# Three cross attentions: stacked rounded parts for the scores, and exponentials made with keys in rows

## The reference

```
q = (x @ Wq + bq) -> [B, H=16, 112, 16]      k, v = ctx_768 @ Wk + bk, @ Wv + bv -> [B, 16, 375, 16]
attn = einsum('bhqd,bhkd->bhqk', q, k) * 16**-0.5
L0_xattn: attn = clip(attn, -10000, 10000)
L1_xattn: attn = where(mask, attn, -finfo.max)
attn = softmax(attn);  x = einsum('bhqk,bhkd->bqhd', attn, v);  out = x @ Wo + bo
L3_xattn: out = relu(x @ W1 + b1) @ W2 + b2
```

## Time and profile before

| | us |
|---|---|
| median of three runs | 1796.17 |
| the profiled execution, span from first to last instruction | 1785.6 |
| what lies around that span, against the median | 10.6 |
| TensorE busy | 1579.5 (88%) |
| TensorE weight loads busy | 1305.9 (73%) |
| VectorE busy | 941.3 (53%) |
| ScalarE busy | 717.5 (40%) |
| GpSimd busy | 409.0 (23%) |
| mean granted TensorE clock | 0.957 of 2.4 GHz |

### The profile page before, as it was taken

The page is one execution under the profiler, slowest core; times in us unless marked ns, Lnnn a source line. Parts: engine busy times, 40 slices in busy tenths (PEclk is TensorE's granted clock), DMA queues, the critical chain, the costliest instruction groups (busy, mean ns, idle before and its releaser), DMA issues.

```text
span 1785.6 us, 40853 instructions
## 1 busy us (share of the span) xinstructions
PE 1579.5 (88%) x14786; PEld 1305.9 (73%) x14786; DVE 941.3 (53%) x2546; ACT 717.5 (40%) x1675; POOL 409.0 (23%) x627
## 2 busy tenths in 40 slices
PE   7998998799987879998797788997988999899998
PEld 6876776678975657776687566775876777689897
DVE  3665877511116657777110562556345667565864
ACT  3334876232323336652222314551755556211110
POOL 2224776500004421112000233432121111000101
PEclk9998999999998999998899798998998999999999
DMA  5343000278951011102686001001001000033232
GB/s 212 147 151 121 28 27 19 106 279 300 321 185 35 1 53 44 29 15 87 254 290 228 13 1 58 28 27 48 1 1 66 23 26 15 24 96 117 81 108 68
DMA packets 41852, 166.72 MB, mean 93 GB/s; under 512 B 5985, under 2 KB 16865, under 8 KB 30177
## 3 DMA queue, kind: packets, MB, share of 16 engines
q1 hardware_dynamic: 39392, 159.14, 25.7%
q0 software_dynamic: 2304, 5.51, 1.0%
HBM read 140.21 MB, written 24.41 MB: 92 GB/s over the span
## 4 chain that ended last, share of the span: by engine, by line
PE 70%; DVE 12%; issue 7%; DMA 3%; POOL 3%; ACT 3%; SPq 1%; DVEq 0%; POOLq 0%; ACTq 0%
PE bank L1688 7%; PE bank L1701 6%; PE bank L1268 6%; PE bank L1630 4%; PE bank L1255 4%; PE bank L1631 4%; PE bank L1632 4%; PE bank L1282 3%; PE bank L795 2%; PE bank L804 2%; PE bank L1238 2%; PE bank L1243 2%; PE bank L896 1%; PE bank L782 1%; DMA xrow<-slots 1%
## 5 line engine op out<-in xcount | busy, mean ns | idle before, releaser
L2053 ACT ACTIVATE arena<-big,nm 112x375 f32<-112x375 f32 x384 | 215.9, 605 | 29.5 <-DVE nm L2894 16.4
L1268 PEld LDWEIGHTS bank<-cst,arena 112*125 112x125 f32 x1152 | 146.6, 192 | 54.0 <-issue 29.0
L1268 PE MATMUL bank<-cst,arena 112*125 112x112 f32 x1152 | 168.0, 283 | 8.8 <-ACT big L2063 5.0
L3150 POOL TENSOR_TENSOR mv<-mv,cst 112x1 f32<-112x1 f32 x88 | 20.1, 228 | 607.3 <-DVE mv L2283 607.3
L2202 ACT ACTIVATE htile<-bank,wup 128x128 f32<-128x128 f32 x280 | 79.7, 368 | 189.7 <-PE bank L1688 189.6
L1688 PE MATMUL bank<-xtile,wup 128*128 128x128 f32 x1120 | 132.8, 278 | 0.3 <-DVE xtile L2997 0.2
L1688 PEld LDWEIGHTS bank<-xtile,wup 128*128 128x128 f32 x1120 | 129.8, 194 | 1.0 <-DVE xtile L2997 0.9
L3013 DVE COPY yrow<-bank 128x256 f32<-128x256 f32 x35 | 14.8, 424 | 217.5 <-PE bank L1701 217.5
L1701 PE MATMUL bank<-wdn,htile 128*128 128x256 f32 x560 | 126.3, 379 | 0.0
L2897 DVE TENSOR_SCALAR_CACHE_REDUCE big<-bank 112x375 f32<-112x375 f32 x192 | 96.0, 543 | 35.3 <-PE bank L1255 33.6
L1701 PEld LDWEIGHTS bank<-wdn,htile 128*128 128x128 f32 x560 | 103.9, 190 | 12.8
(11 more groups left out here) (359 smaller groups left out, 3571.7 us busy)
## 6 DMA issues: line engine op xcount, KB each, us to landing
wup<-in_moe_up SPq DMA_DIRECT2D x35, 1028.0 KB, 7.3
wdn<-in_moe_dn SPq DMA_DIRECT2D x35, 1024.0 KB, 6.1
vspace<-in_ring SPq DMA_DIRECT2D x40, 512.0 KB, 4.2
ctxs<-parts SPq DMA_DIRECT2D x30, 564.0 KB, 3.9
slots<-mlpw SPq DMA_DIRECT2D x11, 1024.0 KB, 6.5
parts<-ctxs SPq DMA_DIRECT2D x8, 564.0 KB, 3.1
xrow<-slots SPq DMA_DIRECT2D x35, 128.0 KB, 5.0
slots<-yrow SPq DMA_DIRECT2D x35, 128.0 KB, 7.0
```

The costliest lines, as they stand in the source:

```text
L1268: mm = pe.transpose(bank[4 + (3 * g + t) % 2][0:KT, j * T:(j + 1) * T], c_pr[:, g, j, t * KT:(t + 1) * KT], ident[0:T, 0:T])
L2053: nc.scalar.activation(c_pr[:, g, j, :], c_sc[:, g % 2, j, :], ACT.Exp, bias=nm[:, p, h:h + 1], scale=-1.0).then_inc(cexp_done, 1)
```

## The change

For these three stages:

- Queries and keys are split into a rounded part (float32r) and the remainder. The rounded part is made by ScalarE (`q_high`, `k_high`), the remainder by GpSimd (`q_low`) and VectorE (`k_low`).
- SyncE copies the parts by DMA, on chip, into stacks with the four heads' 32 rows side by side in time and three blocks of rows: queries high, low, high against keys high, high, low. That is 12 transfers for the keys and 12 for the queries of each batch (13 for the keys with the mask, whose row is row 96).
- Scores are made twice. With queries in rows (L1338 in the new kernel): one float32r matmul of 96 or 97 rows for each head, two heads at a time into one pair of banks, only for the maxima (L2977, one reduce over 2 x 375). The maxima are split too, turned (L1347), and multiplied into rows 96 to 104 of the query stack (`joined`). With keys in rows (L1357): for each tile of 125 keys two float32r matmuls of 105 rows and 224 columns, which give scores minus maxima already turned.
- ScalarE takes the exponentials straight from PSUM (three of 125 x 448 for each group) to where the value products read them. The 12 transposes and the copies go.
- In the clip stage the exponentials are clipped to [exp(-60), 1], two tiles by GpSimd and one by VectorE.
- The keys and values of batch b + 1 and the queries of b + 2 are made in batch b; those of batch 0 all come before the first scores. The copy of the output out of PSUM goes from VectorE to ScalarE. A value product now belongs to `back[2]`, not `back[3]`.
- GpSimd fills constant rows of the stacks at the start of each stage (9 x 3008 twice, with the mask also 1 x 1792 twice).

Core of the diff (the moved order of the steps is shown by rows below it):

```diff
+            def stack_keys(sub, b, p):
+                sp.wait_ge(ckl_done, at(sub, "k2", b, 2))
+                sp.wait_ge(ct_ready, at(sub, "c12", b - 2, 12))
...
+                for i in range(4):
+                    for r, part in enumerate((0, 0, 1)):
+                        sp.dma_start(k_st[32 * r:32 * r + 32, p, :, :]....bitcast(F32),
+                                     k_hl[32 * i:32 * i + 32, part, :, :].bitcast(F32)).then_inc(kst_in, 16)
...
+                if not sub.qk_norm:
+                    stack_keys(sub, 0, 0)
+                    stack_queries(sub, 0, 0)
                 next_weights(SUBS[sub.index - 1])
...
+                    if not sub.qk_norm:
+                        stack_queries(sub, b0 - 1, 1)
                     load_context(sub, b0, 0, False)
+                    if not sub.qk_norm:
+                        stack_keys(sub, b0 - 1, 1)
+                        stack_queries(sub, b0, 0)
...
-                def scores(b, g, p):
...
-                        rows = slice(32 * j, 32 * j + 32)
-                        pe.matmul(bank[j][0:T, 0:S2], c_qm[rows, p, g // 2, g % 2, :], c_kT[rows, p, g // 2, :],
-                                  start=True, stop=True).then_inc(cs_ready, 1)
+                def scores(b, g, p, half):
+                    if g == 0 and half == 0:
+                        pe.wait_ge(qst_in, queries_stacked(sub, b))
+                        pe.wait_ge(kst_in, keys_stacked(sub, b))
+                    pe.wait_ge(cmax_ready, at(sub, "p8", b, 2 * g + half))
+                    for e in range(2):
+                        mm = pe.matmul(bank[e][0:T, 0:S2P], q_st[0:rows, p, 2 * g + half, e * T:(e + 1) * T],
+                                       k_st[0:rows, p, 2 * g + half, :], start=True, stop=True)
+                    mm.then_inc(cs_ready, 1)
+                def shifts_t(b, g, p):
...
+                    pe.transpose(bank[2][:, 0:T], x_nm[:, g % 2, :].bitcast(F32), ident[0:T, 0:T]).then_inc(cx_ready, 1)
+                def scores_t(b, g, p, t):
...
+                    pe.wait_ge(cexp_done, at(sub, "c12", b, n - 1))
+                    for k in range(2):
+                        mm = pe.matmul(bank[4 + n % 2][0:KT, 2 * T * k:2 * T * (k + 1)], k_st[0:SHIFTS, p, 2 * g + k, t * KT:(t + 1) * KT],
+                                       q_st[0:SHIFTS, p, 2 * g + k, :], start=True, stop=True)
...
+                def exps(b, g, p, t):
...
+                    nc.scalar.activation(x_pt[:, g % 2, t, :], bank[4 + n % 2][0:KT, 0:4 * T], ACT.Exp).then_inc(cexp_done, 1)
...
+                def maxima(b, g, half):
+                    dve.wait_ge(cs_ready, at(sub, "p8", b, 2 * g + half + 1))
+                    dve.tensor_reduce(nm[:, g % 2, 2 * half:2 * half + 2], pair[0:T, :, 0:S2], AX_X, ALU.max, negate=True)\
+                        .then_inc(cmax_ready, 1)
...
+                def joined(b, g, p):
+                    dve.wait_ge(cx_ready, at(sub, "g4", b, g + 1))
...
+                nc.gpsimd.memset(k_st[96:SHIFTS, 0, :, :].bitcast(F32), 1.0).then_inc(xset, 1)
```

More of the change, by code:

```diff
@@ L1359, in step @@
-                        if two and sub.mlp:
+                            if not one:
+                                pe.wait_ge(ckl_done, at(sub, "k2", b, 2))
+                            elif sub.mlp:
+                                pe.wait_ge(cq_done, at(sub, "c1", b + 1, 1))
+                            else:
+                                pe.wait_ge(cv_done, at(sub, "c3", b, 3))
+                            keys(b + 1, 1 - p, 0, bank[3])
+                    if g == 1 and more:
+                        pe.wait_ge(ckl_done, at(sub, "k2", b + 1, 1))
+                        keys(b + 1, 1 - p, 1, bank[3])
@@ new lines, in step @@
+                    if g == 2 and more:
+                        pe.wait_ge(ckl_done, at(sub, "k2", b + 1, 2))
+                        value_rows(b + 1, 1 - p, 0, bank[3])
+                    if g == 3:
+                        if more:
+                            pe.wait_ge(cv_done, at(sub, "c3", b + 1, 2 if sub.mlp else 1))
+                            value_rows(b + 1, 1 - p, 2 if sub.mlp else 1, bank[3])
+                        if two and one and not sub.mlp:
+                            idle(b, 2)
+                            pe.wait_ge(con_step, at(sub, "t2", b, 0))
+                            rows_t(sub, b - 2, p)
@@ L1360, in step @@
+                    if back[0]:
+                        scores(b, g, p, 1)
+                    if back[2] and not sub.clip:
+                        values(*back[2])
+                    if back[1]:
+                        scores_t(*back[1], 0)
+                        scores_t(*back[1], 1)
+                    if g == 0 and two:
+                        if not one:
+                            idle(b, 1)
+                        if sub.mlp:
                             hidden(b - 2)
-                        elif two:
-                            if not one:
-                                idle(b, 1)
+                        else:
@@ new lines, in step @@
+                        if after and not sub.mlp:
+                            if two:
+                                y_taken(b - 2)
+                            q_in(b + 2, TL)
+                    if g == 2:
+                        if one:
+                            idle(b, 2)
+                            if sub.mlp:
+                                if two:
+                                    y_taken(b - 2)
+                            elif after:
+                                pe.wait_ge(cq_done, at(sub, "c1", b + 2, 1))
@@ L1449, in step @@
-                        if back[3] and not sub.mlp:
-                            values(*back[3])
-                        if one and not sub.mlp:
-                            idle(b, 1)
-                            output_columns(sub, b - 1)
+                        if after and sub.mlp:
+                            pe.wait_ge(cv_done, at(sub, "c3", b + 1, 3))
+                            q_in(b + 2, bank[3])
+                    if back[2] and sub.clip:
+                        values(*back[2])
@@ L2923, in step @@
-                    if back[0]:
-                        scores_in(b, g, p, (0, 1))
+                    after = more and (not isinstance(b, int) or b + 2 < B)
+                    y_at = 2 if sub.mlp else 1
+                    if back[0]:
+                        maxima(b, g, 0)
+                    if back[1]:
+                        joined(*back[1])
+                    if back[2] and sub.clip:
+                        clipped(*back[2])
                     if two and g == 0 and sub.mlp:
                         output_columns(sub, b - 2)
-                    if two and g == y_at + 2:
+                    if two and g == y_at:
+                        residual(sub, b - 2, p)
@@ L2937, in step @@
[L2937 to L2944 removed]
+                        maxima(b, g, 1)
+                        shifts(b, g, p)
+                    if g < 2 and more:
+                        k_low(b + 1, 1 - p, g, bank[3])
```

699 lines of the change are left out of this document (359 added, 340 removed).

## The result

The changed kernel takes 1976.6 us (median of four runs) against 1795.9 for the kernel before: a ratio of 1.102, 95% interval 1.098 to 1.105. It is slower by 181 us where 14 less were forecast; the range ended at 1825. In the profiled executions the span went from 1785.6 to 1975.0.

A forecast was written before the change was run, and what follows sets the result against it. TensorE (88% busy) was taken to set the steady time, GpSimd the new clip stage; steady batches -45, starts +45 and ends -14 us gave -14 from 1796.2, so 1782 us, range 1750 to 1825.

The forecast's parts named there:

- TensorE's steady work: Steady batches: 2.4 us less where nothing else bounds, 1.4 from replaced matmuls and transposes, 1.0 from fewer waits.
- SyncE's queue: Steady part: 24 transfers a batch at 0.5 us an issue, between rows of 0.34 and 0.65, priced at nothing.
- the slack: Steady part: the next batch's keys need 8.5 us against two steps and a bit, 8.8.
- The starts: Starts of the three stages: first scores wait behind 24 issues, then batch 0 takes 15.4 us; +45 us in all.
- The ends: After each stage's last scores: a shorter chain, half the saving counted, 4.5 us each; -14, bounds -5 and -22.
- GpSimd's clip: Clip stage: 1.85 us for 448 columns, so GpSimd's 18.9 us a batch bounds it and the gain is 1.7.
- L3314's row: Old kernel's GpSimd profile row, 1545 ns for 375 elements with a pointer, used to price the new clip.
- Rival B: Next batch's scores wait for key stacks, transfers over 32 partitions getting half the rate; 1831 us, chance 0.19.
- its point of decision: Key transfers in the steady part: stacks come late from about 0.52 us for each transfer.
- Chances of 0.58 for faster: Whole kernel: faster 0.58, from the cheap-transfer case and most of the forecast; same 0.12, slower 0.30.

## Why the prediction was wrong, point by point

- **TensorE's steady work: the sum right, by luck.** Forecast 2.4 us less for a batch, 1.4 of it work and 1.0 waits. Without stacks a mask batch takes 18.7 us against 20.2, which is 1.5 less, and an mlp batch 20.1 against 23.5, which is 3.4 less: 4.9 for the pair, as the 4.8 that were forecast, but neither of the two alone. The split was off too. Busy time fell by 2.8 and 3.0 us of a batch, twice the forecast, in the main since the matmuls of 224 columns start 0.11 us apart and not 0.15; idle time rose by 1.3 in mask and fell by 0.3 in mlp. In clip no gain was left: 22.9 us against 20.6, where 18.9 was forecast.
- **SyncE's queue: the failed step.** "I take 0.5 for these, between the two", "It just fits and I price it at nothing". It failed threefold. The price: 0.65 us an issue. I took a value between two rows, neither of which was of such a transfer; that the one was also 0.65 was chance (above). The sum: I set the keys' twelve issues against the slack, and the queries' twelve stand ahead of them, because both buffers come free at the same moment, after step 0. A count over one batch would have said it: 5.9 + 24 x 0.65 + 2 = 23.5 us against 18. The order: the mask row behind the queries, and VectorE's in-order read of it, was not looked at in the steady part at all. What the runs showed in place of the "nothing" is a loop of 25.6 us in the changed kernel's clip stage, and an order that cost the mask stage 5 us a batch more. The steady batches missed the forecast by 97 + 38 = 135 us. Moving the context and the mask row gave 38 back (8 of them in the mask stage's batch 0), and halving the count of issues in the five late batches another 61; of the rest, clip's clips hold some 3 us a batch, and the stacks of batches 1 and 2 were left whole.
- **The starts: right in kind, 85 us and not 45.** The first scores came 3 to 3.5 us later than forecast in each stage (172.0 against 168.9 in clip), the price of the issue again. The larger part is batch 0: 23.7, 32.1 and 24.5 us where I had 15.4, since batch 1's stacks come late by the same loop (in clip its key issues end at 194.08 and its scores start at 195.72). I had priced the queue at the start and forgot it one batch later.
- **The ends: wrong, +7.5 and not -14.** Layer norms and routing may fill those steps, as I half allowed; no run tests it.
- **GpSimd's clip: wrong by a factor of three, in the good direction.** 583 ns in the mean for 448 columns, forecast 1.85 us from L3314's row. The 0.67 that I had estimated from the Trainium skill (GPSIMD Engine Reference, elementwise side-by-side cycle accounting), and set aside for that row, was the nearer one. The row was of an operation with a pointer, the new one has constants; that this makes the difference isn't tested. So GpSimd does not bound the stage (16.8 of 46.9 us busy). VectorE is busy for 20 of a 23 us batch, where I had summed 16.2: its holds beside GpSimd were no term of the sum.
- **Rival B: the right place, the wrong mechanism and a quarter of the price.** Its sign came true, the scores wait for the keys' transfer at step 0, and its point of decision (0.52 us for a key transfer) was passed, at 0.65. But half of the bytes gave 10 us at most and half of the count 61, so the reason is the issue and not 32 partitions. Chances of 0.58 for faster were far too high for a forecast that "just fits" on a queue whose price stood between two rows of other transfers, a factor of two apart.

## What to carry to other kernels

Count a queue as an engine: issues in a batch times the price of an issue in a run, plus the time until its buffer is free, plus the landing; compare that loop with the batch before anything else. When work moves to a queue, list what already stood on it: a tiny transfer behind the new ones can hold an in-order engine, and the trace then books the wait to that engine. Where something "just fits", price the case that it does not. Before you average a run of four, read its single instructions, and do not take the price of an issue from a transfer of another shape. The same holds for means of a group: two held instructions of eight can be all that matters.

## What the runs showed of the hardware that I had not expected

- Issues of 94, 56 and 47 KB between partition blocks of 32 cost the queue the same 0.60 us median (about 0.65 from start to start in a run), on SyncE as on ScalarE (0.617); loads of 376 KB from DRAM onto 32 partitions, with four times as many rows, cost 0.61. A context load onto 128 partitions costs 0.34, a store of 752 KB 0.38.
- Three loads of 376 KB onto 32 partitions each were complete only 6.4 us after the last was issued, with the DMA engines full at 214 GB/s; twelve of 94 KB after 1.7.
- GpSimd clamps 125 x 448 with two constants in 0.56 us (median; 0.55 to 0.70); with a pointer operand 112 x 375 took 1.545.
- Beside GpSimd's work single VectorE instructions are held: steps of 4 columns take 0.38 or 1.0 us in place of 0.17, a clip of 448 columns 1.72 in place of 0.39, a layer norm step 3.19 in place of 0.41. Others of the same lines in the same batches take their short time.
